# Eight-batch decoder on one core: the tokens after the recurrence taken in blocks of 16 time steps of all batches instead of 128-step halves of one batch

## The chip, the cores and the metric

The program runs on one core of one Trainium2 chip. The metric is device time in microseconds from start to end of one execution. TensorE (PE) does matrix products into PSUM, VectorE (DVE), ScalarE (ACT) and GpSimd (POOL) do the rest, SyncE (SP) starts the DMA transfers. Engines wait for each other only on semaphores, and each engine takes its instructions in the written order.

## The reference

The program is a decoder of two layers on x of 8 batches x 256 steps x 128 channels, with a context of 8 x 512 x 128. The change is in the second layer, from the recurrence on:

```
# x3: the tokens after layer 0, (8, 256, 128)
u = x @ Wi.T + bi;  sp = x @ Ws.T + bs
state = tanh(state @ A.T + u_t @ B.T) + sp_t;  y_t = state @ C.T      # 256 steps, one after the other
x4 = layernorm(x3 + ys @ Wo.T + bo)
q' = relu(layernorm(x4 @ wq) * gamma + beta) + 1e-6                   # 16 heads of 8 channels
att = q' (k'^T v) / (q' . sum k' + 1e-6)                              # per batch and head
att = att as (heads, steps, 8) read as (steps, 128)                   # "shuffle": no transpose back
x5 = layernorm(x4 + layernorm(att @ dense_w + dense_b) * gamma + beta)
out = layernorm(x5 + fp8(x5 * s) @ fp8(weight * s2).T / (s*s2) + bias)   # s from max |x5| of ALL tokens
```

Two things matter for the order of the work. The shuffle takes head h, steps 16 j to 16 j + 15 (of 8 channels each) as row 16 h + j of the dense map's input, so a block of 16 consecutive steps of all 8 batches gives exactly 128 complete rows. And the last step needs the maximum over all x5 before it can begin.

## The kernel before

Everything is f32 unless marked. Layer 0 fills the program up to the recurrence. There the tokens lie channels on partitions, in order of step, 8 batches side by side (`x3_t`, `hid`: column 8 t + b). The names in the trace are those of the underlying buffers: `prob` is `hid` or `x3_t` (also `mixed` and, later, x5), `pt` holds the folded weights, `score_banks` the pre-activations `cf`, `psum` and `lat` are small SBUF tiles of the stage, `v` holds x4 (`f_all`), `on` the attended tokens `att`, `km` and `ksm` the key-value matrices and the key sums, `out_bank` is `ob`.

**The recurrence.** PE's `step(t)` is two matmuls of 8 columns (L1773), one for each half of the output channels, and ACT's tanh (L850) follows; 255 steps in a strict chain. Behind each step PE issues a piece of other work: in the first 36 steps `z_third` (L1761, L1764, L1767, a third of the pre-activations of 16 later steps, in two halves of 64 output channels; the third third has only one row in each operand) and else `keep_clock`, a matmul of 192 (or 96) columns whose result nobody reads (L1709).

**First half of the steps (`early`).** After step 128 the first 128 tokens of each batch are complete. `early(b, i)` takes batch b during 16 steps: at step i = 1 the output map (L1783, L1784, full width, the moving operand picks every 8th column), at i = 3, 7, 15 transposes (L1371), i = 9 the query map (L1794), i = 16 attention (L1802, L1803). DVE does the layer norms (`statistics`: L919, L922; POOL gives 1/sqrt, L546, L548; L933), the affine map and relu (L1224, L1247), and the division (L1249 to L1251).

**After the recurrence.** The other 128 tokens of each batch go through the same maps in two groups of four batches (L1837 to L1861, DVE L1276 to L1282). SP then stores the attended tokens of each batch in DRAM in the shuffled order (`store_attended`, L492, elements of 32 bytes) and reads them back in two transfers (L506). PE, ACT and DVE take the 16 tiles of 128 rows through the dense map in four fours (L1875, `dense`, `residual`, `normalize_x5`), and L1317 reduces the maximum of x5. From there the fp8 map and the last layer norm follow (L1333 to L1354, stores L512), POOL having added the last bias to x5 in one piece (L675).

## Time and profile before

| | |
|---|---|
| three runs | 1171.66, 1177.38, 1177.3 us (median 1177.3) |
| profiled execution | 1171.73 us, span 1170.0 us from first to last instruction |
| granted TensorE clock, mean | 0.918 of 2.4 GHz |
| busy | PE 965.3 us, DVE 688.5, ACT 503.5, POOL 464.8 |

The profile is of one execution: its span leaves 1.73 us outside. A busy PE says little, since during the recurrence most of its busy time is `keep_clock`. What counts is the order of events from the first tanh at 894.7 us to the end. In a timeline row the first number is the start, the second the duration in us, then engine, line, operation, what is written from what, shape, count; the bracket is the idle time of that engine ahead of the row and what ended it.

### The profile page before, as it was taken

What the parts mean: (1) busy time and instruction counts of PE and PEld (TensorE: products, weight loads), DVE (VectorE), ACT (ScalarE), POOL (GpSimd) and SP (SyncE); (2) the same over time, 40 slices, a digit from 0 to 9 for tenths busy, and PEclk for the clock granted to TensorE, in tenths of its full rate; (3) what the DMA queues carried; (4) which work ended last, traced back from release to release, by engine and by line L of the source; (5) the groups of instructions that cost most, each with busy time, mean ns of one, the idle gap of its engine ahead of it and who ended that gap; (6) DMA issues with size and microseconds to landing.
All of it is one profiled execution on the core that took longest, in us unless ns stands there. A gap on an engine that the chain in (4) does not pass through costs nothing.

```text
span 1170.0 us, 19759 instructions
## 1 busy us (share of the span) xinstructions
PE 965.3 (83%) x7491; PEld 646.7 (55%) x7491; DVE 688.5 (59%) x1903; ACT 503.5 (43%) x1398; POOL 464.8 (40%) x532
## 2 busy tenths in 40 slices
PE   3758999999999998999999999998558999996311
PEld 2435656666666666666656666565336655654211
DVE  3346577567758757667675876765562003445598
ACT  3735645654664664555466365433102333331000
POOL 1134466356356546536645644655410001111041
PEclk8789999999999999899999999999858999997655
DMA  6000000000000000000000000000000000010401
GB/s 172 19 1 6 11 1 6 11 1 6 11 1 6 10 1 1 6 10 1 6 10 2 1 1 1 1 19 1 0 1 2 2 1 6 6 8 3 54 0 36
DMA packets 56812, 12.85 MB, mean 11 GB/s; under 512 B 40318, under 2 KB 56462, under 8 KB 56590
## 3 DMA queue, kind: packets, MB, share of 16 engines
q1 hardware_dynamic: 56718, 11.58, 4.7%
q8 instruction: 60, 0.98, 0.4%
q14 instruction: 34, 0.28, 0.1%
HBM read 9.46 MB, written 2.12 MB: 10 GB/s over the span
## 4 chain that ended last, share of the span: by engine, by line
PE 60%; DVE 22%; ACT 6%; POOL 5%; issue 3%; DMA 2%; SPq 1%; POOLq 0%; DVEq 0%
PE score_banks L1611 8%; PE out_bank L1583 7%; PE bank_d L1709 6%; PE bank_a L1371 5%; PE score_banks L1390 5%; DVE o_rec L1082 4%; PE score_banks L1773 4%; DVE prob L1110 3%; PE score_banks L1415 3%; PE bank_d L1466 3%; PE out_bank L1566 3%; PE score_banks L1392 3%; PE score_banks L1391 3%; PE out_bank L1591 2%; DVE stats L919 2%
## 5 line engine op out<-in xcount | busy, mean ns | idle before, releaser
L799 ACT ACTIVATE prob<-score_banks 128x1024 f32<-128x1024 f32 x128 | 131.1, 1024 | 166.0 <-PE score_banks L1611 165.7
L1611 PE MATMUL score_banks<-qh,kr 64*128 64x256 f32 x1024 | 149.2, 411 | 3.0 <-ACT qh L767 2.6
L636 POOL TENSOR_TENSOR psum<-psum,prob 128x512 f32<-128x512 f32 x64 | 81.5, 1274 | 153.7 <-DVE prob L1110 153.6
L546 POOL TENSOR_TENSOR var_eps<-mv,epsilons 128x2 f32<-128x2 f32 (+2 forms) x64 | 12.7, 198 | 314.3 <-DVE mv L922 314.3
L1082 DVE RECIPROCAL o_rec<-out_bank 128x256 f32<-128x256 f32 x64 | 111.9, 1748 | 28.6 <-PE out_bank L1591 28.6
L1583 PE MATMUL out_bank<-prob,v 128*64 128x256 f32 x1024 | 124.6, 385 | 1.3 <-DVE on L1083 1.3
L634 POOL TENSOR_TENSOR psum<-prob 128x512 f32<-128x512 f32 x64 | 83.1, 1298 | 102.6 <-DVE prob L1110 102.6
L1611 PEld LDWEIGHTS score_banks<-qh,kr 64*128 64x128 f32 x1024 | 91.2, 191 | 42.0 <-issue 32.7
L739 ACT ACTIVATE prob<-prob,neg_max 128x128 f32<-128x128 f32 (+1 forms) x256 | 107.0, 425 | 13.0 <-DVE neg_max L982 13.0
L1110 DVE TENSOR_SCALAR prob<-prob 128x1024 f32<-128x1024 f32 x128 | 101.3, 791 | 17.7 <-ACT prob L799 17.7
L1709 PE MATMUL bank_d<-w_qkv_t,ident 128*64 128x192 f32 (+1 forms) x430 | 105.7, 332 | 0.0
L919 DVE BATCH_NORM_STATS2 stats<-bank_d 128x6 f32<-128x128 f32 x96 | 22.6, 287 | 125.7 <-PE bank_d L1371 93.0
L1583 PEld LDWEIGHTS out_bank<-prob,v 128*64 128x64 f32 x1024 | 67.8, 136 | 46.6 <-issue 17.2
L850 ACT ACTIVATE prob<-score_banks 128x8 f32<-128x8 f32 x255 | 45.3, 178 | 104.8 <-PE score_banks L1773 103.4
L1371 PE MATMUL bank_a<-ident,prob 128*128 128x128 f32 x400 | 66.7, 291 | 28.5 <-DMA prob<-att_scratch 17.9
L1044 DVE TENSOR_TENSOR k_cos<-score_banks,cos_t 128x512 f32<-128x512 f32 x56 | 38.2, 683 | 81.5 <-PE score_banks L1392 44.3
L612 POOL TENSOR_TENSOR kr<-k_cos,k_sin 128x512 f32<-128x512 f32 x64 | 82.8, 1293 | 8.1 <-DVE k_sin L1046 8.1
L638 POOL TENSOR_TENSOR psum<-psum,prob 128x512 f32<-128x512 f32 x64 | 81.6, 1275 | 3.9
L1773 PEld LDWEIGHTS score_banks<-prob,pt 128*64 128x64 f32 x1020 | 52.1, 134 | 54.6 <-ACT prob L850 48.4
L1466 PE MATMUL bank_d<-km,q 64*128 64x128 f32 (+1 forms) x512 | 56.5, 342 | 23.9 <-DVE row_max L977 20.5
L1773 PE MATMUL score_banks<-prob,pt 128*64 128x8 f32 x1020 | 75.3, 212 | 0.7 <-ACT prob L850 0.3
L690 ACT ACTIVATE pt<-bank_a 128x512 f32<-128x512 f32 x96 | 57.3, 597 | 42.0 <-PE bank_a L1371 40.8
(363 smaller groups left out, 2014.5 us busy)
## 6 DMA issues: line engine op xcount, KB each, us to landing
cb<-in_ctx_dram SPq DMA_DIRECT2D x8, 256.0 KB, 2.9
bias_mask<-bias_scratch SPq DMA_DIRECT2D x1, 1536.0 KB, 7.3
xb<-in_x_dram SPq DMA_DIRECT2D x8, 128.0 KB, 2.1
prob<-in_L_xattn_Wkv_dram SPq DMA_DIRECT2D x1, 1024.0 KB, 6.7
att_scratch<-on SPq DMA_DIRECT2D x16, 64.0 KB, 3.3
prob<-att_scratch SPq DMA_DIRECT2D x2, 512.0 KB, 4.0
out_dram<-v SPq DMA_DIRECT2D x4, 256.0 KB, 2.3
prob<-in_L_xattn_Wq_dram SPq DMA_DIRECT2D x1, 512.0 KB, 7.8
```

Of the source, the lines that this page charges most:

```text
L612: g.tensor_tensor(kr[:, key % 2, :], k_cos[:, :], k_sin[:, :], ALU.add).then_inc(kr_ready, 1)
L634: link(g.tensor_tensor(psum[:, p % 2, :], pp[:, 0, :], pp[:, 1, :], ALU.add))
L739: last = s.activation(pr, pr, ACT.Exp, bias=neg_max[:, qt, j, g:g + 1], accum_out=row_sum[:, qt, j, g:g + 1])
L799: s.activation(prob[:, p % 2, 2 * u:2 * u + 2, :].rearrange("p k (h q) -> p h k q", h=2), sc[:, 0:2, :].rearrange("p h (k q) -> p h k q", ...
L1082: link(w.reciprocal(o_rec[:, :], bank[:, T:2 * T]))
L1110: w.tensor_scalar(pr, pr, float(np.exp(-CLIP)), float(np.exp(CLIP)), ALU.max, ALU.min).then_inc(clamped, 1)
L1371: return nc.tensor.transpose(out_ap, in_ap, ident[0:in_ap.shape[0], 0:in_ap.shape[0]])
L1466: last = mm(bank[:, lo:lo + k.stop - k.start], q0[rows_of, q], km[rows_of, jj, k], start=True, stop=True, skip_group_check=True)
L1583: mm(o[DH * h:DH * (h + 1), 0:T], v[:, (q // 2) % 2, kb, lo:lo + DH], prob[:, q % 2, kb, T * h:T * (h + 1)], start=(kb == 0), stop=(kb == ...
L1611: last = mm(sc[:, h, k * T:(k + 1) * T], kr[rows_of, p % 2, kb * P:(kb + 1) * P], qh[rows_of, p % 2, :], start=True, stop=True, skip_group ...
L1709: mm(bank_d2[0:HALF_ROWS, 0:columns], ident[:, 0:HALF_ROWS], w_qkv_t[:, 0:columns], start=True, stop=True, skip_group_check=True)
L1773: last = mm(cf[lo:lo + HALF_ROWS, t * B:(t + 1) * B], a_t[:, lo:lo + HALF_ROWS], hid[:, (t - 1) * B:t * B], start=False, stop=True, skip_g ...
```

## The change

The 256 steps are cut into 16 windows of 16 steps. The 128 tokens of a window (16 steps of 8 batches, contiguous columns) go through all stages beside the recurrence, each stage a fixed number of windows and steps later. PE's work in window k, behind step i: i = 0 and 1 the output map of the window before (inputs, bias row, then states), with tokens now on the output partitions, so that the transpose after it goes; 2 to 5 attention of the window before that, two batches at a time, 16 columns each; 6 dense map (window k - 4); 7, 8, 11, 15 transposes; 9 query map. Every matmul is written as two of 64 output partitions (`halves`), transposes too (plain matmuls with the identity). `keep_clock` runs only in steps without window work. The affine map and relu of the queries work on the transposed tile, where gamma and beta are per-partition scalars; the denominator is one column per head (16) instead of one per channel (128), so `ksm` goes. Each window is stored contiguously by SP and read back with 32-byte elements (`mixed`), one pair of transfers per window. POOL applies gamma and beta of the dense map's norm. x4 is also stored in DRAM and read back in the shuffled row order (`x4_rows`), 16 transfers at the end of the recurrence; x5 and the output have that row order.

After the last step what is left is: the stages of windows 14 and 15, the residual and norm of all of x5 on DVE in four fours, and the fp8 part as before, with POOL's bias in four pieces. The code ahead of the recurrence is unchanged but for the bias (a 1-row product of two matmuls in place of one), two more column loads and the product for `ksm`.

```diff
@@ SP
-            for b in range(B):
-                sp.wait_ge(att_ready, b + 1)
-                store_attended(b, 0)
...
-                for b in range(per * k, per * (k + 1)):
-                    store_attended(b, 1)
...
+            for k in range(1, WINDOWS + 2):
+                if k - 1 < WINDOWS:
+                    sp.wait_ge(x4_ready, k)
+                    sp.dma_start(x4_dram[k - 1], x4[:, k - 1, :]).then_inc(x4_out, 16)
+                if k >= 2:
+                    w = k - 2
+                    sp.wait_ge(att_ready, w + 1)
+                    sp.dma_start(att_dram[w], att[:, w, :]).then_inc(att_out, 16)
+                    sp.wait_ge(att_out, 16 * (w + 1))
+                    sp.wait_ge(mixed_in, 16 * w)
+                    sp.dma_start(mixed[:, w, :].rearrange("p (i e) -> p i e", e=HD),
+                                 rows(att_dram, (HD, P), w * P * D, [(B * D, WINDOW_STEPS), (1, HD)]),
+                                 allow_slow_non_contiguous=True).then_inc(mixed_in, 16)
+                if k == WINDOWS - 1:
+                    sp.wait_ge(x4_out, 16 * (WINDOWS - 1))
+                    for b in range(B):
+                        early = slice(H * b, H * b + H - 1)
+                        sp.dma_start(x4_rows[early, :, :], x4_of_batch[b, 0:H - 1]).then_inc(x4_rows_in, 16)
+                if k == WINDOWS:
+                    sp.wait_ge(x4_out, 16 * WINDOWS)
+                    for b in range(B):
+                        sp.dma_start(x4_rows[last_rows[b], :, :], x4_of_batch[b, H - 1:H]).then_inc(x4_rows_in, 16)
@@ POOL
+            for k in range(1, WINDOWS + 3):
+                if k - 1 < WINDOWS:
+                    rstd_of_window(W_X4, EPS_LN, x4_var, x4_rstd, k)
+                if k >= 4:
+                    scale_dense(k - 4)
+                if k - 1 < WINDOWS:
+                    rstd_of_window(W_Q, 1e-6, q_var, q_rstd, k)
+                if k >= 4:
+                    finish_dense(k - 4)
@@ ACT
+                if i == 6 and 0 <= k - 2 < WINDOWS:
+                    s.activation(att_t, ob[:, 0:P], ACT.Identity).then_inc(att_t_ready, 1)
+                if i == 8 and 0 <= k - 1 < WINDOWS:
+                    s.activation(x4_t, bank_a[:, 0:P], ACT.Identity).then_inc(x4_t_ready, 1)
+                if i == 12 and 0 <= k - 3 < WINDOWS:
+                    s.activation(mixed_t, bank_a[:, 0:P], ACT.Identity).then_inc(mixed_t_ready, 1)
@@ DVE
+            for k in range(1, WINDOWS + 3):
+                new = k - 1 < WINDOWS
+                if 0 <= k - 2 < WINDOWS:
+                    rectify_queries(k - 2)
+                if new:
+                    measure_window(W_X4, bank_d[:, 0:D], x4_var)
+                    normalize_window(W_X4, x4[:, k - 1, :], bank_d[:, 0:D]).then_inc(x4_ready, 1)
+                if k >= 4:
+                    measure_dense(k - 4)
+                if 0 <= k - 2 < WINDOWS:
+                    divide_attended(k - 2)
+                if new:
+                    measure_window(W_Q, bank_d[:, 0:D], q_var)
+                if k >= 4:
+                    normalize_dense(k - 4)
+                if new:
+                    normalize_window(W_Q, q1, bank_d[:, 0:D]).then_inc(q_ready, 1)
...
+            for step, k in ((add_rows, 0), (add_rows, 1), (normalize_x5, 0), (add_rows, 2), (measure_dense, 15),
+                            (normalize_x5, 1), (normalize_dense, 15), (normalize_x5, 2), (add_rows, 3)):
+                step(k)
@@ PE
+            def product_of_rows(bank, tokens, weights, **kw):
+                for of in halves:
+                    last = mm(bank[of, 0:D], tokens[:, of], weights, skip_group_check=True, **kw)
+                return last
...
+                if here(k - 1, 0):
+                    inputs_of(k - 1)
+                elif here(k - 1, 1):
+                    states_of(k - 1)
+                elif 2 <= i <= 5 and 0 <= k - 2 < WINDOWS:
+                    attend(k - 2, i - 2)
+                elif here(k - 4, 6):
+                    dense(k - 4)
...
+            for t in range(1, T):
+                step(t)
+                k, i = divmod(t, WINDOW_STEPS)
+                worked = window(k, i)
...
+            for t in range(T, T + 4 * WINDOW_STEPS):
+                window(*divmod(t, WINDOW_STEPS))
```

On PE, behind step 128 before: the first steps of one batch of `early`. L1773 is the step, L1709 `keep_clock`.

```order
L1773 MATMUL score_banks<-prob1,pt 64x8 x4
L1783 MATMUL bank_a<-prob1,pt 128x128
L1784 MATMUL bank_a<-prob,pt 128x128
L1773 MATMUL score_banks<-prob1,pt 64x8 x2
L1709 MATMUL bank_d1<-w_qkv_t,ident 64x192
L1773 MATMUL score_banks<-prob1,pt 64x8 x2
L1371 MATMUL bank_d0<-ident,psum 128x128
L1773 MATMUL score_banks<-prob1,pt 64x8 x2
L1709 MATMUL bank_d1<-w_qkv_t,ident 64x192
```

On PE now, behind steps 0 to 6 of a window in the second half of the recurrence (L1810 is the step, L1823 `product_of_rows`, L1846 and L1850 `attend`; `sin_t` is the row of ones):

```order
L1823 MATMUL bank_d0<-pt,prob 64x128 x2
L1823 MATMUL bank_d0<-x_t,sin_t 64x128 x2
L1810 MATMUL score_banks<-prob1,pt 64x8 x2
L1823 MATMUL bank_d0<-pt,prob1 64x128 x2
L1810 MATMUL score_banks<-prob1,pt 64x8 x2
L1846 MATMUL out_bank<-psum,km 64x16 x4
...
L1850 MATMUL out_bank<-head_mask,psum 64x16 x2
L1810 MATMUL score_banks<-prob1,pt 64x8 x2
L1823 MATMUL bank_d1<-w_dense,psum 64x128 x2
L1823 MATMUL bank_d1<-b_dense,sin_t 64x128 x2
```

The full-width products of every 8th column have become pairs of halves on contiguous columns; two pairs per window have a single row in each operand. All other PE work ahead of a step is shorter than before.

On DVE now, behind the last step, from the residual of the first four tiles on (L1336 the residual, L967 and L970 statistics, L981 and L1344 norm and maximum of x5, L1275, L1276, L1279 the dense norm of window 15; `bias_mask` is `x4_rows`):

```order
L1336 TENSOR_TENSOR bias_mask<-bias_mask,prob 128x512
L967 BN_STATS stats<-bias_mask 128x6 x4
L970 BN_AGGR mv<-stats 128x2 x4
L1275 BN_STATS stats<-bank_d 128x6
L1276 BN_AGGR mv<-stats 128x2
L981 TENSOR_SCALAR prob<-bias_mask,mv,rstd 128x128 x4
L1344 TENSOR_REDUCE small<-prob 128x1
L1279 TENSOR_SCALAR prob<-bank_d,mv,rstd 128x128
L981 TENSOR_SCALAR prob<-bias_mask,mv,rstd 128x128 x4
L1344 TENSOR_REDUCE small<-prob 128x1
```

Three residuals and one norm of x5 stand ahead of window 15's dense statistics in DVE's order, where before all of the dense stage came after the transfers back.

On SP now, from window 15 on: the transfers that follow each other on its queue (L517 and L521 the stores, L524 the read back with 32-byte elements, L531 and L535 `x4_rows`; `x_scratch` is the store of x4):

```order
L524 DMA prob<-att_scratch 128x16x8 [waits mixed_in,att_out]
L531 DMA bias_mask<-x_scratch 15x16x128 [waits x4_out]
L531 DMA bias_mask<-x_scratch 15x16x128 x7
L517 DMA x_scratch<-v 128x128 [waits x4_ready]
L521 DMA att_scratch<-on 128x128 [waits att_ready]
L524 DMA prob<-att_scratch 128x16x8 [waits mixed_in,att_out]
L535 DMA bias_mask<-x_scratch 1x16x128 [waits x4_out]
L535 DMA bias_mask<-x_scratch 1x16x128 x7
L521 DMA att_scratch<-on 128x128 [waits att_ready]
L524 DMA prob<-att_scratch 128x16x8 [waits mixed_in,att_out]
```

The last window's store and read back stand behind two sets of eight transfers that are new.

## Rows read from the trace of the kernel before

**Rows 1.** Busy time by stretch: recurrence in two parts, to x5's maximum, rest.
```profile
span 1170.0 us, 19759 instructions
895.00:970.20 75.20, 74.92 (x916) 48.08 (x917) 0.00 (x0) 22.94 (x129) 0.00 (x0) 1.00 0.01 2
970.20:1050.90 80.70, 80.11 (x763) 48.22 (x762) 33.09 (x100) 27.75 (x149) 11.71 (x32) 1.00 0.09 7
1050.90:1137.10 86.20, 34.23 (x132) 24.69 (x132) 56.83 (x178) 6.43 (x11) 16.94 (x25) 0.65 0.16 19
```

**Rows 2.** Timeline: last tanh, and the maximum of x5.
```profile
1050.66 0.18 ACT L850 ACTIVATE prob<-score_banks 128x8 f32<-128x8 f32 x1 [0.39 <-PE score_banks L1773]
...
1134.83 2.27 DVE L1317 TENSOR_REDUCE small<-prob 128x1 f32<-128x2048 f32 x1
```

**Rows 3.** Timeline of early steps: pair of halves, one-row pair, keep.
```profile
895.09 0.42 PE L1761 MATMUL score_banks<-prob,pt 128*64 128x128 f32 x4
...
895.34 0.33 PE L1709 MATMUL bank_d<-w_qkv_t,ident 128*64 128x96 f32 x2
...
896.08 0.29 PE L1773 MATMUL score_banks<-prob,pt 128*64 128x8 f32 x4
...
896.30 0.43 PE L1767 MATMUL score_banks<-sin_t,rec_t 1*64 1x128 f32 x4
...
897.16 0.18 ACT L850 ACTIVATE prob<-score_banks 128x8 f32<-128x8 f32 x1 [0.57 <-PE score_banks L1773]
```

**Rows 4.** Timeline of batch 0 in the second half: product, transpose, attention.
```profile
969.71 0.71 PE L1783 MATMUL bank_a<-prob,pt 128*128 128x128 f32 x2
...
971.15 0.18 ACT L850 ACTIVATE prob<-score_banks 128x8 f32<-128x8 f32 x1 [1.14 <-PE score_banks L1773]
...
971.64 0.33 PE L1371 MATMUL bank_d<-ident,psum 128*128 128x128 f32 x1
...
972.28 0.18 ACT L850 ACTIVATE prob<-score_banks 128x8 f32<-128x8 f32 x1 [0.39 <-PE score_banks L1773]
...
980.13 0.18 ACT L850 ACTIVATE prob<-score_banks 128x8 f32<-128x8 f32 x1 [0.81 <-PE score_banks L1773]
```

**Rows 5.** Timeline: one layer norm of 128 tokens, ACT copy, reciprocal.
```profile
972.01 0.30 DVE L919 BATCH_NORM_STATS2 stats<-bank_d 128x6 f32<-128x128 f32 x1 [83.26 <-PE bank_d L1371]
...
973.46 0.41 DVE L933 TENSOR_SCALAR x<-bank_d,mv,rstd 128x128 f32<-128x128 f32 x1 [0.93 <-POOL rstd L548]
...
974.62 0.27 ACT L835 ACTIVATE psum<-bank_a 128x128 f32<-128x128 f32 x1
...
1052.31 0.95 DVE L1250 RECIPROCAL o_rec<-o_rec 128x128 f32<-128x128 f32 x1
```

**Rows 6.** Transfers: landing times by group (page), and four issues in a row.
```profile
att_scratch<-on SPq DMA_DIRECT2D x16, 64.0 KB, 3.3
prob<-att_scratch SPq DMA_DIRECT2D x2, 512.0 KB, 4.0
...
w_dense<-in_L_xattn_dense_w_dram SPq DMA_DIRECT2D x1, 64.0 KB, 2.4
...
1087.05 3.93 SPq L492 DMA_DIRECT2D att_scratch<-on  x4
```

**Rows 7.** Timeline of the dense stage: residual, statistics, rstd, norm, bias.
```profile
1110.39 0.69 DVE L1300 TENSOR_TENSOR cn<-cn,v 128x512 f32<-128x512 f32 x1
...
1112.02 0.38 DVE L922 BATCH_NORM_AGGREGATE mv<-stats 128x2 f32<-128x6 f32 x4
...
1112.77 1.01 POOL L548 TENSOR_TENSOR rstd<-var_eps,minus_half 128x4 f32<-128x4 f32 x1
...
1116.82 1.09 DVE L933 TENSOR_SCALAR prob<-cn,mv,rstd 128x128 f32<-128x128 f32 x4
...
1134.67 4.50 POOL L675 TENSOR_TENSOR x<-prob,b_ffn 128x2048 f32<-128x2048 f32 x1 [1.30 <-DVE prob L933]
```

**Rows 8.** Timeline: eight keep_clock matmuls of 192 columns at the half clock.
```profile
885.07 4.72 PE L1709 MATMUL bank_d<-w_qkv_t,ident 128*64 128x192 f32 x16
```

More of the change, by code:

```diff
@@ L417, in decoder @@
         FIRST_LOADS = 8
-        SETUP_LOADS = 18
+        SETUP_LOADS = 20
         @block.sync
@@ L669, in _, with rstd_of_window @@
-            for k in range(0, 8, 4):
-                for i, eps in enumerate((1e-6, 1e-6, EPS_LN, EPS_LN)):
-                    rstd_of(late, k + i, 4, eps, half=i % 2)
-            late += 8
-            pool.wait_ge(x2_ready, B + 4)
-            g.tensor_tensor(x2[:, 0:NT, :], x5[:, :, :], b_ffn[:, :].unsqueeze(1).broadcast_to([P, NT, D]),
-                            ALU.add).then_inc(x5b_ready, 1)
+            def rstd_of_window(at, eps, var, done, count):
+                pool.wait_ge(var, count)
+                link(g.tensor_tensor(var_eps[:, at:at + 1], mv[:, at, 1:2], epsilons[:, EPSILONS.index(eps), 0:1],
+                                     ALU.add))
+                g.tensor_tensor(rstd[:, at:at + 1], var_eps[:, at:at + 1], minus_half[:, 0:1],
+                                ALU.pow).then_inc(done, 1)
@@ new lines, in add_bias @@
+            def add_bias(k):
+                part = slice(4 * k, 4 * k + 4)
+                pool.wait_ge(x5_ready, k + 1)
+                g.tensor_tensor(x2[:, part, :], x5[:, part, :], b_ffn[:, :].unsqueeze(1).broadcast_to([P, 4, D]),
+                                ALU.add).then_inc(x5b_ready, 1)
+            for k in range(3):
+                rstd_of(norms + 8, k, 4, EPS_LN, half=k % 2)
+                if k == 1:
+                    add_bias(0)
+            scale_dense(WINDOWS - 1)
+            finish_dense(WINDOWS - 1)
@@ L1303, in normalize_x5, with measure_window @@
-            def normalize_x5(k):
-                t = (t4, t4b)[k % 2]
-                dve.wait_ge(rstd_ready, late + 4 * (k // 2) + 2 + k % 2 + 1)
-                normalize([x5[:, 4 * k + i, :] for i in range(4)], tiles_of(t, 4), k % 2).then_inc(x2_ready, 1)
-                dve.wait_ge(x2_ready, B + k + 1)
-            for step, k in ((dense, 0), (dense, 1), (residual, 0), (residual, 1), (normalize_x5, 0), (dense, 2),
-                            (normalize_x5, 1), (dense, 3), (residual, 2), (residual, 3), (normalize_x5, 2),
-                            (normalize_x5, 3)):
+            def measure_window(at, tile, ready):
+                link(w.bn_stats(stats[:, at, :], tile))
+                w.bn_aggr(mv[:, at, :], stats[:, at, :]).then_inc(ready, 1)
@@ L1806, in _, with turn_halves @@
-            for t in range(1, P):
+            halves = [slice(0, HALF_ROWS), slice(HALF_ROWS, P)]
+            def turn_halves(bank, tile):
+                for of in halves:
+                    last = mm(bank[of, 0:P], tile[:, of], ident[:, :], start=True, stop=True, skip_group_check=True)
+                return last
+            def product_of_rows(bank, tokens, weights, **kw):
+                for of in halves:
+                    last = mm(bank[of, 0:D], tokens[:, of], weights, skip_group_check=True, **kw)
+                return last
@@ new lines, in attend @@
+            def attend(k, part):
+                if part == 0:
+                    pe.wait_ge(kvm_ready, 1)
+                    pe.wait_ge(q1_ready, k + 1)
+                    if k >= 1:
+                        pe.wait_ge(att_ready, k)
+                q_by_batch = q1_t.rearrange("p (i b) -> p b i", b=B)
+                for b in (2 * part, 2 * part + 1):
+                    for of in halves:
+                        mm(ob[of, 0:P].rearrange("p (i b) -> p b i", b=B)[:, b], kvm[:, b, of], q_by_batch[:, b],
+                           start=True, stop=True, skip_group_check=True)
+                if part == 3:
+                    for of in halves:
+                        last = mm(ob[of, P:P + H], k_weighed[:, of], head_mask[:, :], start=True, stop=True,
+                                  skip_group_check=True)
+                    last.then_inc(att_t_full, 1)
```

411 lines of the change are left out of this document (170 added, 241 removed).

## The prediction

> **What bounds the kernel now.** I read the busy time by stretch first. From the first tanh to the last the program takes 155.9 us in two parts [rows 1]: 127 steps in 75.2 us and 128 steps in 80.7 us, at the full clock. Then come 86.2 us to the maximum of x5, in which PE is busy for 34 us and DVE for 57: neither is full, this is a chain of stages that wait for each other. The remaining 32.9 us (1170.0 - 1137.1) are the fp8 map, which the change leaves alone. Exactly, the last tanh ends at 1050.84 and the reduction at 1137.10, 86.3 us later [rows 2]. Next I read the steps themselves. A step without trouble has ACT idle for 0.39 us and then 0.18 us of tanh, so a period of 0.565 us, with a keep_clock or a transpose behind it (the tanh at 972.28) [rows 4]. This latency (PE, ACT, two semaphores) is the floor; work behind a step is free as long as PE is done with it in time. The second half is above the floor because of two places per batch: the output map at i = 1 makes ACT idle for 1.14 us in place of 0.39, attention for 0.81 [rows 4]. 80.7 - 128 x 0.565 = 8.4 us, about 1.05 per batch.
>
> **The recurrence after the change.** The prices come from the first steps [rows 3]. A pair of halves on 128 contiguous columns lets the next matmul start 0.25 us later (895.09 to 895.34) and ends 0.42 after its start; the step itself takes about 0.14 of PE's order. So a pair behind a step needs 0.39 of 0.565: free. That covers i = 1, 7, 8, 9, 11 and 15. Attention takes four small matmuls behind a step (six at i = 5), of 16 columns where the step's two have 8, so 0.25 to 0.4 us: free too. The pair with one row in each operand is dearer: 0.43 us itself, and the period there is 0.75 (ACT idle 0.57). I take 0.43 for it; i = 0 then needs 0.14 + 0.25 + 0.43 = 0.82, so 0.27 over the floor, and i = 6 the same. That is 15 + 12 places x 0.27 = 7.3 us. In windows 1 and 2 the thirds share steps with window work: about ten places at 0.1 and one or two at 0.3, 1.3 us. The twelve one-row thirds stay, 12 x 0.18 = 2.2. Sum: 255 x 0.565 + 2.2 + 7.3 + 1.3 = 154.9 us against 155.9: **-1.0 us**. What was won by contiguous operands (the product at 969.71 needed 0.71 us for 128 picked columns) is given back by the one-row pairs.
>
> A rule bears on this. The row says that a full-width transpose between two half-width steps costs nothing (971.64, and the next period is the floor [rows 4]), so I credit nothing for its removal. The Trainium skill, page "TensorEngine Tiling (Array Packing)", Key Properties, says that changing the tiling mode, not just the tile, drains TensorE; by that rule the 6 full-width places in each of 8 batches would have cost two drains each, and with 0.09 us for one (half of the 0.18 above) their removal would bring 8.6 us more and a time near 1111. The one-row pairs, which change the mode as well, agree with it.
>
> **Waits inside a window.** PE takes its instructions in order, so a late tile stops the recurrence itself. The stages: a norm of 128 tokens takes 1.86 us from statistics to result (972.01 to 973.87, POOL's part included), an ACT copy 0.27 [rows 5]. x4: pair ends 0.56 after step 1, norm ready at 2.6, its transpose stands at i = 7, 3.9 us after: cover 1.3. Query map at i = 9 needs ACT's copy, which follows tanh 8: about 0.1 too late at worst, inside the slack of a pair. Queries: product ends 0.7 after step 9, the division of the attended tokens (three short operations, 0.8 us; a reciprocal of 128 columns is 0.95 and now has 16) stands ahead of it on DVE, so ready at 2.8; the transpose is at i = 15, 3.5 us after: cover 0.7. Relu: after i = 15 three DVE operations, 1.1 us, ready 1.75 after; attention starts 2.1 after: cover 0.35, the thinnest. Read back: the division ends 1.4 us after step 8, then a store of 64 KB in long rows (the like of it lands after 2.4 [rows 6]), 0.5 of issue, and a read of 32-byte elements (the store of such elements lands after 3.3). 7.6 us; it is needed at i = 11 of the next window, 11.4 us after: cover 3.8. So no wait is in my sum; these covers are the rivals' doors. POOL has 3.3 us of work in a window of 9.6, DVE about 4.7.
>
> **After the last step.** The clock stays full for the first few us and then falls, as it did before (mean 0.65 [rows 1]); I give later pairs 0.6 us. From the end of the last tanh:
> - output map of window 15: 0.25 + 0.43 + 0.42 = 1.1; norm, to 3.0; transpose, copy, query map, to 4.3; division of window 14 and norm of the queries, to 6.5.
> - transpose 0.6, relu 1.1, attention (18 small matmuls) 1.5, copy 0.3, transpose 0.6, division 0.8: 11.4, with semaphores 11.7.
> - store and read back 6.3: 18.0. Transpose, copy, dense map with its one-row pair (0.6 + 0.35 + 1.2): dense tile of window 15 at 20.2.
> - Window 14 is ahead: divided at 4.7, stored and read back by 11 (the eight 120 KB transfers of x4 rows go out just before; 1 MB in two transfers landed after 4.0 us each [rows 6], so about 1 us more), 12. Dense map and norm to 16.
> - Then DVE alone counts. One residual with statistics takes 2.0 us (1110.39 to 1112.40), rstd on POOL 1.4 (to 1113.78), a norm of four tiles 1.09 [rows 7], and a quarter of the maximum 0.57 [rows 2], so 1.7 with it. In its order: 2.0 + 2.0 + 1.7 + 2.0 = 7.7, to 23.7 (window 15's tile has been there for 3.5 us: the read back is hidden), 0.5 + 1.7 + 0.4 + 1.7 + 2.0 + 1.4 + 1.7 + 0.3 = 9.7, to **33.4**. POOL's quarters of the bias (4.50 / 4 = 1.1 each [rows 7]) lie beside it.
>
> Before it was 86.3: **-52.9 us**. Gone are the products of four batches, the full-width reciprocals, sixteen scattered stores on one queue (four issues take 3.93 us [rows 6]), and of the dense stage all but the residuals.
>
> **Setup and end.** One more pair of one-row products ahead of the recurrence, +0.3; the product for `ksm` lay beside other work on DVE. The fp8 part is the same. Sum: 1170.0 - 1.0 - 52.9 + 0.3 = 1116.4 us span, with the 1.7 us outside 1118. The profiled execution lies at the low end of the three, 5.6 us under the median; I take 1120 for the median.
>
> **Bounds.** One-row pair behind a step: between 0 (all hidden) and 0.5 over the floor: -7 to +6 us. Landing of a transfer with 32-byte elements: 2.4 (the fastest like it) to about twice 3.3; for window 14 that moves DVE's start by -1 to +4. If window 15 decides, from 20.2 on, at least 30 us: -3.5. Together 1110 to 1130 for this case.
>
> **Rivals.**
> 1. *Waits in the windows.* Three covers are under 0.8 us (i = 2, 9, 15). If each is missed by 0.3 us, that is 0.9 x 15 = 14 us: 1132. For it: semaphore latencies are only roughly in my sums, DVE's order is rigid, and POOL is passed twice per norm. Against: the like chains in the second half of before made no step later, except at the two heavy products.
> 2. *The clock falls in the windows.* Behind 12 of 16 steps keep_clock is gone, and i = 2 to 5 have only small matmuls. At the half clock eight keep_clock matmuls take 4.65 us, 0.58 each [rows 8], which with the step no longer fits a period. With every PE term doubled a window is 4 x 0.86 + 10 x 0.78 + 2 x 1.64 = 14.5 us in place of about 9.7: +4.8 each. In all 15 windows 72 us: 1190, slower than before; it decides from the eleventh such window on (52.9 / 4.8). In four windows: 1138. Against it: PE was 99% busy in both parts of the recurrence with pieces of like size, and transposes that are now plain products add work. The Trainium skill, page "TensorE: Matmul & The Clock Gate" ("What's actually happening"), says that the clock follows how busy the array has recently been and that half rate is the default; by that rule this change is exposed at i = 2 to 5. No stretch of before's recurrence is that thin, so no row decides it.
> 3. *The tail is shorter still*, because window 14 comes back earlier or one-row pairs hide: 1111.
>
> **Chances.** Forecast 0.62; more than forecast 0.08; waits 0.18; clock in some windows 0.07; in all 0.05. The range 1110 to 1138 leaves out the last and the ends. A measurement of this kernel can tell about 0.5% (6 us) from no change. Faster 0.94, same 0.01, slower 0.05.
>
> **What would show it.** The granted clock in the recurrence at 1.00; ACT's idle time ahead of tanh 0.39 in 13 or 14 of 16 steps, 0.6 to 0.75 behind i = 0 and 6; PE waiting for h_ready alone; 155 us from first to last tanh; the last tanh to the end of the reduction 31 to 36 us, DVE without a gap from the first residual to the last statistics; about 33 us after that. Wrong it would be by idle time of PE that ends with DVE or a DMA inside the windows, by a clock under 1.00 there, or by DVE waiting for window 15's dense tile.

## The result and the profile after

Four executions took 1147.91, 1146.47, 1150.76 and 1146.83 us, median 1147.4, beside 1177.3 for the kernel before: ratio 0.9755, 95% interval [0.9712, 0.9799]. The change gains 2.4%, but only half of what I had forecast (1120, range 1110 to 1138). The profiled execution took 1147.91 us with a span of 1146.1, so 23.9 us less span than before. One execution of a later kernel (fill_one_load) took 2115 us where its other three took 1126 to 1130, and is left out.

The busy time by stretch of the kernel after, cut at the same events as [rows 1]: recurrence in two parts, then to the maximum of x5.

```profile
901.60:950.00 48.40, 47.90 (x724) 38.06 (x725) 11.07 (x38) 13.93 (x79) 5.14 (x15) 0.86 0.09 13
950.00:1075.60 125.60, 124.32 (x1684) 89.13 (x1682) 48.59 (x172) 38.51 (x219) 36.24 (x94) 0.76 0.15 20
...
1075.60:1114.10 38.50, 12.68 (x150) 7.68 (x148) 25.99 (x89) 1.66 (x6) 18.21 (x32) 0.61 0.34 37
```

The column to look at is the granted clock, the third from the end: 0.86 and 0.76 in the recurrence, where before it was 1.00 in both parts. PE's busy time tells nothing of it: 124.3 of 125.6 us. The events that answer to [rows 2], in the timeline of the kernel after:

```profile
1075.40 0.18 ACT L902 ACTIVATE prob<-score_banks 128x8 f32<-128x8 f32 x1 [0.39 <-PE score_banks L1810]
...
1113.88 0.16 DVE L1356 TENSOR_REDUCE small<-small 128x1 f32<-128x4 f32 x1
```

So the spans are accounted for in four parts. The first tanh starts at 901.63 in place of 894.72: +6.9. From the first tanh to the last it takes 173.8 us in place of 155.9: +17.8. From the end of the last tanh (1075.58) to the end of the maximum (1114.04) it takes 38.5 in place of 86.3: -47.8. The rest takes 32.1 in place of 32.9: -0.8. Sum -23.9. Against the 1116.4 us of my sum the places are +18.9 (recurrence, 154.9 forecast), +5.1 (tail, 33.4 forecast), +6.6 ahead of the recurrence and -0.8 behind.

**The recurrence.** The chain of waits from 901 to 1075 us, ACT's and PE's part:

```profile
ACT prob L902 <- PE score_banks L1810: 121.1, 254, 1.3
...
PE score_banks L1810 <- ACT prob L899: 0.3, 1, 0.3
```

ACT waits for PE and PE never for DVE, POOL or a transfer: no tile comes late, and my first rival is out. What happens is seen inside one window. Window 8 in five stretches: work behind i = 1 to 4 (attention from 2 on), 5 to 7, 9 and 10, 11 and 12, and 14:

```profile
990.60:992.90 2.30, 2.19 (x54) 1.65 (x50) 0.96 (x4) 0.71 (x4) 0.74 (x2) 1.00 0.00 0
992.90:994.90 2.00, 1.99 (x41) 1.39 (x38) 0.48 (x2) 0.70 (x4) 0.14 (x1) 1.00 0.14 41
995.50:997.50 2.00, 2.00 (x23) 1.51 (x22) 1.30 (x5) 0.53 (x3) 0.77 (x3) 0.50 0.11 33
997.50:998.90 1.40, 1.40 (x15) 0.98 (x14) 0.41 (x1) 0.52 (x3) 0.92 (x3) 0.68 0.16 10
999.10:999.80 0.70, 0.70 (x12) 0.37 (x9) 0.00 (x0) 0.23 (x2) 0.00 (x0) 1.00 0.94 54
```

The clock goes from 1.00 (2.4 GHz) to 0.50 (1.2 GHz) behind i = 8, shortly after the attention steps and the dense map, and is back less than 4 us later. In most other windows it falls behind i = 5 to 8, in windows 3 and 13 behind i = 4 and 3, and through most of window 6 it is still down from window 5. The steps show the price (timeline of ACT in the same window; the first row is the tanh of i = 8):

```profile
994.95 0.18 ACT L902 ACTIVATE prob<-score_banks 128x8 f32<-128x8 f32 x1 [0.39 <-PE score_banks L1810]
...
996.28 0.18 ACT L902 ACTIVATE prob<-score_banks 128x8 f32<-128x8 f32 x1 [0.49 <-PE score_banks L1810]
997.14 0.18 ACT L902 ACTIVATE prob<-score_banks 128x8 f32<-128x8 f32 x1 [0.68 <-PE score_banks L1810]
...
999.18 0.18 ACT L902 ACTIVATE prob<-score_banks 128x8 f32<-128x8 f32 x1 [0.39 <-PE score_banks L1810]
```

And from window 6, the tanh behind the one-row pair of i = 0 at the half clock:

```profile
968.19 0.18 ACT L902 ACTIVATE prob<-score_banks 128x8 f32<-128x8 f32 x1 [1.28 <-PE score_banks L1810]
```

At the half clock a step with window work behind it has a period of 0.67 us (0.49 + 0.18; 0.85 at i = 5), one with keep_clock 0.86, and one with a one-row pair 1.46, where at the full clock they are 0.565, 0.565 and 0.85. The clock is at the half in part of every window from 2 on (75 of the 173.8 us in all), and windows 2 to 14 take 10.3 to 12.7 us in place of the 9.7 that I had counted.

**The tail.** The timeline of SP and DVE behind the last tanh:

```profile
1074.17 7.94 SPq L531 DMA_DIRECT2D bias_mask<-x_scratch  x8
...
1078.29 0.41 DVE L1279 TENSOR_SCALAR v<-bank_d,mv,rstd 128x128 f32<-128x128 f32 x1 [0.93 <-POOL rstd L692]
...
1082.15 0.56 SPq L517 DMA_DIRECT2D x_scratch<-v  x1
...
1087.02 5.43 SPq L535 DMA_DIRECT2D bias_mask<-x_scratch  x8
...
1093.99 0.69 DVE L1336 TENSOR_TENSOR bias_mask<-bias_mask,prob 128x512 f32<-128x512 f32 x1 [0.40 <-DMA bias_mask<-x_scratch]
```

SP needs 7.94 us to issue the eight transfers of x4 rows. The last x4 tile is ready at 1078.70 and is stored only at 1082.15; the store of window 14's attended tokens behind it goes at 1082.76, ready at 1080.25. The first residual then waits for the last of the second eight and starts 18.4 us after the last tanh; I had DVE start at 16.0. From there to the end of the maximum it is 20.05 us, where I had 17.4. DVE has operations there that take far longer than their like (DVE and POOL together):

```profile
1099.24 1.26 POOL L716 TENSOR_TENSOR x<-prob,b_ffn 128x512 f32<-128x512 f32 x1
1099.53 1.51 DVE L1336 TENSOR_TENSOR bias_mask<-bias_mask,prob 128x512 f32<-128x512 f32 x1
...
1104.89 2.48 DVE L981 TENSOR_SCALAR prob<-bias_mask,mv,rstd 128x128 f32<-128x128 f32 x4
...
1106.03 1.26 POOL L716 TENSOR_TENSOR x<-prob,b_ffn 128x512 f32<-128x512 f32 x1
...
1107.45 1.26 POOL L716 TENSOR_TENSOR x<-prob,b_ffn 128x512 f32<-128x512 f32 x1 [0.16 <-DVE prob L981]
1108.01 1.25 DVE L1336 TENSOR_TENSOR bias_mask<-bias_mask,prob 128x512 f32<-128x512 f32 x1
...
1112.00 1.12 DVE L981 TENSOR_SCALAR prob<-bias_mask,mv,rstd 128x128 f32<-128x128 f32 x4 [1.25 <-POOL rstd L576]
```

The residual at 1099.53 takes 1.51 us in place of 0.69, the one at 1108.01 takes 1.25, and the norm at 1104.89 2.48 in place of 1.1, each with a piece of POOL's bias beside it. That is 0.82 + 0.56 + 1.38 = 2.8 us. Not all of the norm's 1.38 is the bias: POOL's scale by gamma and its add of beta for window 15 (128 columns, 1105.06 to 1106.07) lie beside it too, and in bias_last, where no bias is near, this norm still takes 1.52. So 0.4 goes with gamma and beta and 1.0 with the bias.

### The profile page after: what moved, and what is told of

Same layout as the page of the kernel before. It is cut to its first block, busy times and chain, and to the rows that moved or that the text cites. A ratio compares the mean times of both kernels' runs of the same rounds, so it can differ in the third digit from the quotient of the medians.

```text
span 1146.1 us, 21485 instructions
## 1 busy us (share of the span) xinstructions
PE 966.1 (84%) x8233; PEld 665.1 (58%) x8233; DVE 682.3 (60%) x1923; ACT 500.3 (44%) x1412; POOL 494.0 (43%) x615
## 3 DMA queue, kind: packets, MB, share of 16 engines
q8 instruction: 66, 1.08, 0.4%
## 4 chain that ended last, share of the span: by engine, by line
PE 61%; DVE 20%; ACT 6%; POOL 5%; issue 3%; SPq 3%; DMA 2%; POOLq 0%; DVEq 0%
PE score_banks L1650 8%; PE out_bank L1622 7%; PE bank_a L1410 5%; PE score_banks L1429 5%; PE score_banks L1810 5%; DVE o_rec L1130 5%; DVE prob L1158 3%; PE score_banks L1454 3%; PE bank_d L1505 3%; PE score_banks L1431 3%; PE out_bank L1605 3%; PE score_banks L1430 3%; PE bank_d L1823 3%; PE out_bank L1630 2%; PE score_banks L1749 2%
## 5 line engine op out<-in xcount | busy, mean ns | idle before, releaser
L1158 DVE TENSOR_SCALAR prob<-prob 128x1024 f32<-128x1024 f32 x128 | 101.2, 791 | 18.4 <-ACT prob L851 18.4
L1622 PEld LDWEIGHTS out_bank<-prob,v 128*64 128x64 f32 x1024 | 67.8, 136 | 46.6 <-issue 17.2
L1810 PE MATMUL score_banks<-prob,pt 128*64 128x8 f32 x1020 | 89.7, 228 | 1.8 <-ACT prob L899 0.3
L1810 PEld LDWEIGHTS score_banks<-prob,pt 128*64 128x64 f32 x1020 | 68.1, 163 | 38.8 <-ACT prob L902 27.1
L690 POOL TENSOR_TENSOR var_eps<-mv,epsilons 128x1 f32<-128x1 f32 x48 | 9.1, 189 | 149.8 <-DVE mv L1276 149.8
L1410 PE MATMUL bank_a<-ident,prob 128*128 128x128 f32 x384 | 62.3, 286 | 11.6 <-ACT pt L742 5.4
L1410 PEld LDWEIGHTS bank_a<-ident,prob 128*128 128x128 f32 x384 | 43.1, 142 | 33.5 <-ACT pt L742 17.6
L1505 PEld LDWEIGHTS bank_d<-km,q 64*128 64x128 f32 x512 | 37.3, 203 | 40.8 <-issue 39.0
```

What stands on the lines that cost most here:

```text
L1158: w.tensor_scalar(pr, pr, float(np.exp(-CLIP)), float(np.exp(CLIP)), ALU.max, ALU.min).then_inc(clamped, 1)
L1410: return nc.tensor.transpose(out_ap, in_ap, ident[0:in_ap.shape[0], 0:in_ap.shape[0]])
L1505: last = mm(bank[:, lo:lo + k.stop - k.start], q0[rows_of, q], km[rows_of, jj, k], start=True, stop=True, skip_group_check=True)
L1622: mm(o[DH * h:DH * (h + 1), 0:T], v[:, (q // 2) % 2, kb, lo:lo + DH], prob[:, q % 2, kb, T * h:T * (h + 1)], start=(kb == 0), stop=(kb == ...
L1810: last = mm(cf[lo:lo + HALF_ROWS, t * B:(t + 1) * B], a_t[:, lo:lo + HALF_ROWS], hid[:, (t - 1) * B:t * B], start=False, stop=True, skip_g ...
```

## The experiments

Two theories for the recurrence. **A1:** the steps with only small attention matmuls behind them, four in a row, bring the clock down. **A2 (rival):** it is the missing keep_clock in the other window steps (pairs and transposes). For the tail, **D:** SP's sixteen issues delay window 14 and the residuals; **E:** DVE is slowed while POOL adds the bias. All ran beside the kernel before. After's own ratio is 0.9755.

**fill_attend.** Unread matmuls of 96 columns behind the attention steps alone:

```diff
                 if not worked:
                     keep_clock(KEEP_Z if t <= 3 * Z_PARTS else KEEP, bank_d2 if t < Z_FIRST // B else sc[:, 0, :])
+                elif i in (2, 3, 4, 5) and t > 3 * Z_PARTS:
+                    keep_clock(KEEP_Z, bank_d2 if t < Z_FIRST // B else sc[:, 0, :])
```

> The changed kernel with a keep_clock of 96 columns added behind the four attention steps of each window (i = 2 to 5, 56 steps from step 37 on). Changed kernel: 173.9 us from the first to the last tanh, granted clock falling to half once per window from i = 7 on. Theory A (the clock falls because the attention steps leave TensorE too thinly used): the clock stays at full in most windows, recurrence 156 to 162 us, total 12 to 18 us less. Rival B (the one-row pairs or something else in the window pull it down): recurrence 171 to 174 us, nothing won. Rival C (the clock is not what lengthens the windows, PE is simply short of time behind a step): 174 to 178 us.

1130.1 us (1129.6 to 1132.4), ratio 0.9581 [0.9567, 0.9596]. The windows of its profile that cover the recurrence:

```profile
904.20:952.60 48.40, 48.02 (x784) 35.76 (x784) 12.89 (x45) 15.33 (x87) 7.38 (x20) 1.00 0.09 15
952.60:1060.00 107.40, 106.88 (x1732) 71.15 (x1730) 46.41 (x166) 37.10 (x211) 34.03 (x89) 1.00 0.17 23
```

The clock is 1.00 throughout, with work added. Recurrence 155.5 us, 18.3 less, and just under the 156 to 162 expected. The median is 17.2 us under after's; by the ratios to the kernel before, which ran anew beside each group of kernels, it is 1.7% or 20 us. So the whole excess in the recurrence is the clock. A window takes 9.67 us, with i = 0 and 6 at 0.85 and 0.84, as I had costed them (0.565 + 0.27). The step i = 5, with six small matmuls and the 96 columns, takes 0.63; without the columns, at the full clock, it is at the floor in after. The other five traces with this filler have recurrences of 155.3 to 156.8 us; the two kernels whose recurrence is after's, after itself and x4_one_load, have 173.8 and 170.1.

**fill_all.** The same behind every window step but i = 0 and 6 (`elif i not in (0, 6) and t > 3 * Z_PARTS`).

> As fill_attend, with 96 columns behind every window step but i = 0 and 6 (also 1, 7, 8, 9, 11, 15). Theory A: full clock throughout, every step but two per window at 0.565 us, recurrence 155 to 158 us, total 16 to 18 us less than the changed kernel. If 0.14 + 0.25 + 0.17 us behind a step do not fit 0.565 us after all, 0.03 to 0.1 us more at six steps per window: 158 to 164 us. Rival B: the clock still falls, and with half-rate pairs and more columns each added piece costs 0.2 us: 180 us and more. Rival C: the same, 180 us.

1128.6 us (1126.6 to 1131.0), ratio 0.9566 [0.9547, 0.9584]; recurrence 156.8 us. The clock fell once, in window 2, whose steps 2 to 4 are among the first 36 steps and so have no filler. Filling the other steps gives nothing that can be told from fill_attend.

**fill_pairs.** The same 96 columns, but behind the steps with pairs and transposes (`elif i in (1, 7, 8, 9, 11, 15) ...`) and none behind attention.

> The changed kernel with 96 columns behind the six other steps of a window (i = 1, 7, 8, 9, 11, 15) and none behind the attention steps. More columns are added than in fill_attend (6 in place of 4 per window). Theory A1 (the four thin attention steps in a row are what drops the clock): it still falls once in most windows, recurrence 168 us or more. Theory A2 (what counts is the work of the whole window): full clock, recurrence 155 to 158 us.

1150.5 us (1147.8 to 1154.6), ratio 0.9768 [0.9738, 0.9798]; recurrence 174.4 us. The second part of it in the profile:

```profile
950.00:1075.00 125.00, 123.78 (x1764) 99.95 (x1763) 47.60 (x167) 36.83 (x209) 34.06 (x88) 0.80 0.15 19
```

The clock falls behind i = 5 to 7 of each window from window 5 on. In windows 2 to 4 it does not, where in after it does, and it is down for 51 us in all in place of 75; but a step with added columns then takes 0.96 us at the half clock, and nothing is won. So the filler in the other steps may help a little, and it doesn't hold the clock: what does is the filler behind the attention steps. A1 stands against A2. That it must be four such steps in a row is not shown (in window 13 of after the clock fell behind the second of them).

**before_thin.** The kernel before, without keep_clock at four steps of each batch in the second half:

```diff
-                if i not in PE_EARLY:
+                if i not in PE_EARLY and i not in (4, 5, 6, 8):
```

> The kernel BEFORE with keep_clock left out at i = 4, 5, 6 and 8 of every batch in the second half of the recurrence (32 steps), nothing else. Theory A1 (thin steps in a row drop the clock, whatever else the window has): granted clock falls once per batch, the strided products at half rate, second half 80.7 us -> 90 to 105 us, total 8 to 25 us more. Rival (the changed kernel's other matmuls, halves and transposes as plain products, are what drops it): clock 1.00 throughout, 80.7 us, time unchanged.

1203.9 us (1200.5 to 1205.8), ratio 1.0214 [1.0193, 1.0236]. Its recurrence in two parts:

```profile
902.90:980.00 77.10, 76.63 (x929) 48.99 (x929) 0.00 (x0) 23.66 (x133) 0.00 (x0) 1.00 0.01 2
980.00:1083.50 103.50, 94.22 (x686) 71.70 (x685) 33.09 (x100) 26.98 (x146) 11.75 (x32) 0.58 0.07 5
```

The clock falls in the old kernel too, from nothing but work taken away, and 25.6 us more is just past the 8 to 25 expected. Here it does not come back in each batch: it is down from 982.7 to 1016.8 and from 1023.7 to 1071.5 us, and five of eight batches take 14.0 to 14.1 us in place of 10.3. Nearly all of their steps are longer, those with keep_clock 0.85, those with attention and with the full-width output map 1.59 and 1.53 us where they take 1.0 and 1.32 at the full clock. PE's busy share did fall here, to 91% of the second part. So the new matmul shapes are not needed to bring the clock down; thin steps alone do it.

**no_bias_rows.** This kernel leaves out the bias of the output map and of the dense map, and with them both one-row pairs of each window.

```diff
-                product_of_rows(bank_d, one_row[:, 0:P], bias_row, start=False, stop=False)
...
-                product_of_rows(bank_d2, one_row[:, 0:P], b_dense[0:1, :], start=False, stop=True)...
```

> The changed kernel without the one-row pairs: the bias of the output map and of the dense map is left out. Theory A: the clock still falls once per window; only the 27 dear steps shrink (0.28 us each at full clock, 0.8 at half): recurrence 163 to 167 us. Rival B (one-row pairs pull the clock down): full clock, recurrence 147 to 150 us.

1135.3 us (1130.1 to 1136.5), ratio 0.9613 [0.9590, 0.9636]; recurrence 161.7 us, 12.1 less than after and under the 163 to 167 expected. The steps i = 0 and 6 are at the floor where the clock is full, so the pair costs 0.28 each there, 7.6 us for 27 places; the other 4.5 us go with what they cost more at the half clock and with windows without a fall, but after and x4_one_load differ by 3.7 us with the same recurrence, so that part is rough. The second part in the profile:

```profile
950.00:1060.00 110.00, 108.48 (x1516) 79.82 (x1514) 44.64 (x160) 35.86 (x204) 32.36 (x84) 0.76 0.16 21
```

The clock still falls in ten windows (10.1 to 10.7 us each, where windows 3, 8 and 13, without a fall, take 9.04 to 9.05), so the one-row pairs are not needed for it.

**x4_one_load.** x4 is stored in the shuffled order and read back by one 1 MB transfer in place of sixteen:

```diff
-                    sp.dma_start(x4_dram[k - 1], x4[:, k - 1, :])...
+                    sp.dma_start(x4_shuffled[:, k - 1].rearrange("b i d -> i b d"), x4[:, k - 1, :])...
-                    for b in range(B):
-                        sp.dma_start(x4_rows[last_rows[b], :, :], x4_of_batch[b, H - 1:H])...
+                    sp.dma_start(x4_rows[:, :, :], x4_shuffled.rearrange("b k i d -> (b k) i d"))...
```

> The changed kernel with x4 stored in DRAM in the shuffled order already (the same 512-byte rows), so that one transfer of 1 MB takes the place of the 16 transfers of x4 rows. Changed kernel: last tanh to the end of the maximum 38.5 us, first residual 18.4 us after the last tanh, stores of windows 14 and 15 held up on SP by 2.5 and 4.0 us. Theory D (SP's issue time of about 1 us for each of the 8, then 0.7 for each of the next 8, is what made the tail late): first residual 2 to 3 us earlier, tail 35.5 to 36.5 us, total 2 to 3 us less, recurrence unchanged. Rival (DVE's order and PE's chain set it anyway): nothing, or later, if the one big transfer lands after 18 us.

1148.7 us (1145.0 to 1152.0), ratio 0.9744 [0.9717, 0.9771], not to be told from after. In its timeline:

```profile
1081.16 1.09 SPq L528 DMA_DIRECT2D bias_mask<-x_scratch  x1
...
1090.81 0.41 DVE L1272 TENSOR_SCALAR prob<-bank_d,mv,rstd 128x128 f32<-128x128 f32 x1 [0.93 <-POOL rstd L685]
1091.13 0.68 DVE L1329 TENSOR_TENSOR bias_mask<-bias_mask,prob 128x512 f32<-128x512 f32 x1
```

The load has landed 5.9 us after 1081.16, by 1087.1. The residual starts at 1091.13, 16.6 us after the last tanh in place of 18.4, and now stands behind window 14's dense norm. Tail 36.7 in place of 38.5, just short of what D had expected (35.5 to 36.5). So D is right in kind, and behind the wait for the transfers stood the next one, for window 14's dense tile. Single traces of the tail with the same code beyond the last step (after, fill_attend, fill_all, fill_pairs) lie between 38.1 and 39.4 us, so gains of 1 to 2 us rest on the rows and not on the sums.

**fill_one_load** is fill_attend and x4_one_load together.

> fill_attend and x4_one_load together: 96 columns behind the attention steps, and one transfer for the x4 rows. fill_attend: recurrence 155.5 us; x4_one_load: last tanh to the end of the maximum 36.6 us where the changed kernel has 38.5. If the two add: recurrence 155.5, tail 36.6, about 1.5 to 2 us less than fill_attend, ratio to before 0.955 to 0.957. Rival (the tail gain is lost when the recurrence ends earlier against the last transfers): equal to fill_attend.

Its three executions outside the profile took 1126.0, 1128.1 and 1130.1 us, ratio 0.9574 [0.9552, 0.9596], the same as fill_attend within what can be told. The same kernel again, for its trace:

> The kernel with 96 unread columns behind the attention steps and the x4 rows read back in one transfer, once more, for a usable trace and as the neighbour of the two kernels beside it. Ratio to the kernel before 0.957 (0.955 to 0.960). From the last tanh to the end of the maximum 36.6 us as in the kernel with the one transfer alone, first residual 16.6 us after the last tanh, recurrence 155 to 156 us.

1128.2 us (1127.8 to 1130.2), ratio 0.9593 [0.9567, 0.9619]; recurrence 155.3, first residual 16.9 us after the last tanh, tail 36.9.

**bias_last.** fill_attend with all four of POOL's `add_bias` behind its last 1/sqrt.

> fill_attend, with POOL's four pieces of the last bias moved behind all of its 1/sqrt work. In the changed kernel three DVE instructions that run beside such a piece took 1.51, 1.25 and 2.48 us where the same form takes 0.69 and 1.08 elsewhere. Theory E (DVE is slowed while POOL works on 512 columns of SBUF): the three are 0.69, 0.69 and 1.08, tail (last tanh to maximum) 38.5 -> 35.5 to 36.5 us, and small DVE instructions after the maximum are up to 1 us later: total 1.5 to 3 us less. Rival (the long rows are waits of another kind that the profile counts as busy): tail unchanged, and 0 to 2 us more because the fp8 part waits for the bias.

1131.6 us (1129.1 to 1132.9), ratio 0.9602 [0.9583, 0.9620], no gain, tail 38.4. The slow operations moved (timeline of DVE and POOL):

```profile
1084.70 1.52 DVE L978 TENSOR_SCALAR prob<-bias_mask,mv,rstd 128x128 f32<-128x128 f32 x4
1084.86 0.48 POOL L700 TENSOR_TENSOR prob<-prob,l_g 128x128 f32<-128x128 f32 x1 [0.53 <-DVE prob L1276]
...
1086.85 0.68 DVE L1333 TENSOR_TENSOR bias_mask<-bias_mask,prob 128x512 f32<-128x512 f32 x1
...
1090.21 3.70 POOL L716 TENSOR_TENSOR x<-prob,b_ffn 128x512 f32<-128x512 f32 x3
1090.28 3.98 DVE L978 TENSOR_SCALAR prob<-bias_mask,mv,rstd 128x128 f32<-128x128 f32 x4 [1.25 <-POOL rstd L576]
```

The two slow residuals are back at 0.68, the third norm at 1.52 has only gamma and beta beside it, and the last norm, which now has three pieces of the bias beside it, takes 3.98 us in place of 1.12. The gain that I expected went there: E is right in the rows, and the place was wrong.

**rows_first.** fill_one_load with the first residual ahead of window 14's dense statistics on DVE:

```diff
+                if k == WINDOWS + 2:
+                    dve.wait_ge(x4_rows_in, 16)
+                    add_rows(0)
                 if k >= 4:
                     measure_dense(k - 4)
```

> As its neighbour, but the first residual and its statistics stand ahead of window 14's dense statistics in DVE's order, where DVE had waited 1.5 us for PE (and 0.6 for POOL). Theory D (from the first residual on DVE's own order sets the tail): the residual starts as soon as the one transfer has landed, about 13 to 14 us after the last tanh, and the maximum ends 1.5 to 2 us earlier, 34.8 us after it; ratio about 0.0015 lower than the neighbour's, hardly to be told by the times, but to be read in the rows. Rival: window 15's chain through the transfers sets the end (its dense tile 20 to 22 us after the last tanh and at least 12 us of work behind it): then nothing moves, and DVE waits for window 15's tile.

1128.9 us (1126.0 to 1129.4), ratio 0.9597 [0.9568, 0.9626]. In its timeline:

```profile
1069.70 0.68 DVE L1306 TENSOR_TENSOR bias_mask<-bias_mask,prob 128x512 f32<-128x512 f32 x1
...
1092.02 0.16 DVE L1351 TENSOR_REDUCE small<-small 128x1 f32<-128x4 f32 x1
```

The last tanh ended at 1056.70. The residual starts 13.0 us after it in place of 16.9, the tail is 35.5 in place of 36.9: 1.4 us of the 1.5 to 2 expected, and too small for the times. The residual came 3.9 us earlier and the second one only 2.1, since window 14's statistics with a wait of 0.93 us for POOL stand between them, and the first norm of x5 waits 0.82 for POOL once more. DVE's own order and POOL's 1/sqrt set the end of the tail; window 15's tile is not waited for.

**bias_behind_norms.** rows_first with all of POOL's bias behind the last norm of x5 (`pool.wait_ge(x5_ready, 4)` ahead of the four).

> As rows_first, and POOL adds its four pieces of the bias only behind the last norm of x5, beside the reduction and the fp8 part, where POOL had been idle for 18 us. Theory E (a DVE operation of 128 or 512 columns between SBUF tiles takes two to four times as long while POOL works on 512 columns): residuals at 0.69, norms at 1.1, the tail another 2.5 to 3 us shorter (about 32 us); of that the small operations and the quantising beside the 5 us of bias give back 1 to 5 us, so between 2 us gained and 2 lost in all. Rival (the slow rows have another cause): residual and norm stay at 1.25 to 2.5.

1126.2 us (1124.0 to 1126.8), ratio 0.9569 [0.9543, 0.9595]. In its timeline (last tanh to 1058.05):

```profile
1083.76 1.52 DVE L972 TENSOR_SCALAR prob<-bias_mask,mv,rstd 128x128 f32<-128x128 f32 x4
...
1091.20 0.16 DVE L1349 TENSOR_REDUCE small<-small 128x1 f32<-128x4 f32 x1
...
1092.23 0.79 DVE L1354 TENSOR_SCALAR diag<-ident,diag 2x2 f32<-2x2 f32 x1
...
1094.35 1.10 DVE L1360 TENSOR_TENSOR small<-small 128x1 f32<-128x1 f32 x1
```

The tail is 33.3 us, 2.2 less than in rows_first, where 2.5 to 3 were expected. All residuals take 0.68, the norms 1.09 to 1.11 but one, and two tiny operations on the way to the scale take 0.79 and 1.10 us in place of 0.22 and 0.16, which gives 1.5 back. It has the lowest median of all that ran and beats both kernels of this case. That it beats fill_attend is not shown: the medians differ by 4 us, but by the ratios to the kernel before only 1.4 us are left, fill_all has a ratio as low (0.9566), and the intervals overlap. Against rows_first, which ran beside it, it is 2.7 us lower, and there too the intervals overlap.

The slow rows end with POOL's piece: the tiny operations at 1092.23 and 1094.35 end at 1093.02 and 1095.45, the pieces beside them at 1093.00 and 1095.44. In after the slow residuals end 0.54 and 0.55 us behind POOL's pieces, less than their own 0.69. This looks like waiting for POOL and not like slower work, but no run was made to separate the two.

## Why the prediction was off

- **What bounds it.** Right: a strict chain of steps with a floor of 0.565 us, then a chain of stages. At the full clock the recurrence takes 155.5 us (fill_attend) where my sum said 154.9.
- **The one-row pairs at i = 0 and 6.** Right: 0.27 over the floor forecast, 0.28 measured. The free places (pairs, transposes, attention at i = 2 to 5) were free: in after, from window 3 on and at the full clock, they are at 0.56 to 0.57. The 0.63 at i = 5 of fill_attend is the filler's, about 0.8 us of its 155.5.
- **The recurrence's sum, -1.0 us: this is the step that failed.** It used the full clock for 255 steps ("at the full clock", "free as long as PE is done with it in time"). The run gave +17.8. None of its terms was mis-sized at the full clock; the clock under all of them was not what I took it for. I had the mechanism as rival 2, gave it 0.12 in all, and argued against it with PE's busy share of 99% in before. That share is no evidence: it is 99% in the kernel after too, with the clock at 0.76, and in the first part of before_thin at 1.00. (Where steps are left with nothing behind them, as in the second part of before_thin, it does fall, to 91%.) How little the attention steps give PE to do stood in the diff, and was the evidence. The Trainium skill, "TensorE: Matmul & The Clock Gate" ("What's actually happening"), has the clock follow how busy the array has recently been; fill_attend, fill_pairs and before_thin agree, but its "busy" is not the busy time that the profile prints. I should have given that sentence more weight than the share.
- **The price of a fall.** What came was rival 2 with falls in all windows, which had a chance of 0.05, at a quarter of its price. It had 4.8 us for each window, all of it at the half clock with every term doubled. In fact the clock is down for 3.4 us of the cheapest windows, 6 to 7 of others and 11 of window 6, and a step is then 0.67 to 0.86, not 0.78 to 0.86, and with a one-row pair 1.46, not 1.64: 0.6 to 3.0 us for a window, 18.3 / 14 = 1.3 on average. So falls in all windows did not bring the time back over 1177. "In four windows" was not a case that occurred. (The row has 4.72 us for eight keep_clock matmuls, 0.59 each; the prediction reads 4.65 and 0.58.)
- **Waits in the windows (rival 1).** Right to leave out: no PE wait on DVE, POOL or a transfer.
- **The tail, -52.9 us: right in kind, 5.1 us too much credited.** -47.8 was measured. DVE started 18.4 and not 16.0 us after the last tanh, since the eight issues ahead take SP 7.94 us (I had 1 us for them, from landing times and not from the issue), and DVE's own order took 20.05 and not 17.4, of which 2.8 is DVE beside POOL: "POOL's quarters of the bias lie beside it" was costed at nothing. A quarter of the maximum takes 0.69, not 2.27 / 4 = 0.57. x4_one_load gave 1.8 us of it, rows_first 1.4, bias_behind_norms 2.2, down to 33.3; that this is the forecast 33.4 is luck, since DVE's order is another one there. Window 15's read back was hidden, as forecast.
- **Ahead of the recurrence, +0.3 forecast, +6.9 in the profile.** Mostly not the change's, as far as single traces tell. In the traces of the ten other kernels of this study the first tanh stands between 897.0 and 904.3 us, and in before_thin, whose code up to there is that of the kernel before, at 902.9, which is 8.2 later than in the one trace of before. That trace was early; against the median I had allowed 2 us for this and 5.6 would have been nearer. Why this part varies from run to run is open.
- **The drain rule** that I had weighed: its 8.6 us did not appear, since the recurrence at the full clock took 155.5 us and not about 146. They could not have: my sum already had those places at the floor of 0.565. Whether a change of width costs anything between steps stays undecided: no run put the full-width ones back alone.
- **Rival 3** (a shorter tail, 1111 us) did not occur.

Together: 27.4 us over the forecast of 1120, of which the recurrence is 19 and the tail 5; the remaining 3 to 4 go with where the profiled execution of before lay.

## What to carry to other kernels

Where a chain of small steps holds the clock up by filler work, count what every step gives to TensorE after a change, step by step; the busy share need not warn you (99% before and after here), and four thin steps in each window cost 18 us here, given back by 96 unread columns behind each. When a transfer is cut into pieces, cost SP's issue time for each piece and look what stands behind them on its queue. An operation on another engine is only free beside DVE if DVE's own rows next to it keep their length; moving it helps only if it goes beside work that does not slow down.

## What the runs showed of the hardware

- The granted clock fell to 0.50 and came back to 1.00 inside the 10 us of one window of the program, in window after window, with PE busy 99% of the recurrence (124.3 of 125.6 us). In before_thin it stayed at 0.50 through whole batches.
- At the half clock a strict step grows from 0.565 to only 0.67 us with a product or transpose behind it, and to 0.86 with a keep_clock of 192 columns or the six small matmuls of i = 5. The step with the full-width product of every 8th column grows from 1.32 to 1.53.
- DVE operations slow down beside POOL's 512-column add from SBUF to SBUF: 0.69 to 1.25 and 1.51, 1.52 to 2.48, 1.12 to 3.98, and a 1-column operation from 0.16 to 1.10; the reductions of 512 columns beside it kept their 0.69. Beside POOL's 128-column gamma and beta a norm of four tiles took 1.52 in place of 1.08.
- Issuing a transfer of 240 rows of 512 bytes took SP about 1 us (7.94 for eight), one of 16 such rows 0.68 (5.43 for eight), and one contiguous MB 0.98 to 1.09; the store of 64 KB in long rows landed after 1.5 us and the read of 32-byte elements after 2.9.
